# A GRU on one Trainium2 core: VectorE turns the scaled x of two time steps in one instruction instead of one

## The reference

```python
def step(h, xs):
    xzt, xrt, xht = xs                       # x @ W_z, x @ W_r, x @ W of this time step
    z = sigmoid(xzt + h @ U_z + vz)          # vz, vr, vh: condition @ C_z, C_r, C plus bias
    r = sigmoid(xrt + h @ U_r + vr)
    hh = tanh(xht + r * h @ U + vh)
    h_new = (1.0 - z) * h + z * hh
    return (h_new, h_new)
...
_, out_t = jax.lax.scan(step, h0, xs)
return x + swapaxes(out_t, 0, 1)
```

## Time and profile before

| | us |
|---|---|
| median of three runs | 2360.33 |
| lowest and highest run | 2358.73, 2360.34 |
| the profiled execution's own time | 2360.46 |
| its span, first to last instruction | 2358.3 |

### The profile page before, as it was taken

How to read it: one execution, slowest core, us unless ns; L and a number is a source line. 1 busy time by engine, 2 the same in 40 slices (tenths; PEclk the granted TensorE clock), 3 DMA queues, 4 the chain that set the end, 5 groups by cost and what they waited for, 6 DMA issues and landing times.

```text
span 2358.3 us, 186250 instructions
## 1 busy us (share of the span) xinstructions
PE 2291.0 (97%) x83078; PEld 1886.3 (80%) x83078; DVE 1750.7 (74%) x7717; ACT 1044.5 (44%) x3091; POOL 630.3 (27%) x1165
## 2 busy tenths in 40 slices
PE   2999999999999999999999999999999999999998
PEld 1788878888788887888878888888888888888887
DVE  4777777777777777777777777777777777777776
ACT  2444444444444444444444444444444444444443
POOL 0222222222222222222222222222222222222222
PEclk8999999999999999999999999999999999999999
DMA  9010110110101101101101101111011011011000
GB/s 201 20 36 18 36 36 18 36 36 18 36 24 30 36 19 36 36 18 36 36 19 36 36 18 36 27 27 36 21 33 36 18 36 36 18 36 36 18 18 21
DMA packets 145362, 78.17 MB, mean 33 GB/s; under 512 B 9024, under 2 KB 140608, under 8 KB 145216
## 3 DMA queue, kind: packets, MB, share of 16 engines
q1 hardware_dynamic: 145216, 76.84, 13.6%
HBM read 43.25 MB, written 33.55 MB: 33 GB/s over the span
## 4 chain that ended last, share of the span: by engine, by line
PE 92%; DVE 3%; SPq 2%; ACT 1%; issue 1%; DMA 1%; ACTq 0%; POOLq 0%; POOL 0%; DVEq 0%
PE banks L226 39%; PE p_bank L234 38%; PE banks L256 14%; DVE taken L533 1%; SPq L135 1%; ACT gate_c L363 1%; DVE h_t L539 1%; DVE state L537 1%; DMA u<-in_L_cond_U_dram 1%; SPq L130 0%; ACT L358 0%; PE p_bank L242 0%; SPq L145 0%; ACT L356 0%; ACT gate_r L358 0%
## 5 line engine op out<-in xcount | busy, mean ns | idle before, releaser
L234 PE MATMUL p_bank<-w_hi,x_t 128*32 128x384 f16 x16384 | 1187.7, 326 | 5.1 <-DVE w_lo L452 3.5
L234 PE MATMUL p_bank<-w_lo,x_t 128*32 128x384 f16 x8192 | 710.2, 326 | 0.0
L234 PEld LDWEIGHTS p_bank<-w_hi,x_t 128*32 128x32 f16 x16384 | 481.5, 97 | 146.6 <-issue 6.0
L226 PE MATMUL banks<-u,h_t 128*32 128x128 f32 x16384 | 548.0, 274 | 14.5 <-DMA u<-in_L_cond_U_dram 5.8
L226 PE MATMUL banks<-u,reset_t 128*32 128x128 f32 x16384 | 543.6, 273 | 5.9 <-DVE reset_t L523 4.9
L226 PEld LDWEIGHTS banks<-u,h_t 128*32 128x32 f32 x16384 | 411.9, 109 | 140.8 <-DVE h_t L539 125.2
L226 PEld LDWEIGHTS banks<-u,reset_t 128*32 128x32 f32 x16384 | 428.5, 109 | 91.7 <-DVE reset_t L523 76.0
L198 POOL TENSOR_TENSOR kept<-keep,state 128x128 f32<-128x128 f32 x512 | 234.7, 458 | 896.4 <-ACT keep L360 896.4
L430 DVE SCALAR_TENSOR_TENSOR banks<-p_bank,x_down,base 128x128 f32<-128x128 f32 x1536 | 470.2, 337 | 5.0 <-issue 3.4
L208 POOL TENSOR_TENSOR result<-x_nat,state 128x128 f32<-128x128 f32 x512 | 234.3, 458 | 817.7 <-DVE state L537 817.7
L356 ACT ACTIVATE h_hi<-h_t 128x128 f16<-128x128 f32 x512 | 158.6, 310 | 433.7 <-DVE h_t L539 433.6
(11 more groups left out here) (55 smaller groups left out, 1837.7 us busy)
## 6 DMA issues: line engine op xcount, KB each, us to landing
x_nat<-in_x_dram SPq DMA_DIRECT2D x256, 128.0 KB, 3.1
out_dram<-result SPq DMA_DIRECT2D x256, 128.0 KB, 2.7
w_stage<-in_L_cond_W_r_dram SPq DMA_DIRECT2D x4, 256.0 KB, 5.5
w_stage<-in_L_cond_W_z_dram SPq DMA_DIRECT2D x4, 256.0 KB, 8.3
w_stage<-in_L_cond_W_dram SPq DMA_DIRECT2D x4, 256.0 KB, 10.8
u<-in_L_cond_U_z_dram SPq DMA_DIRECT2D x4, 256.0 KB, 13.6
c_w<-in_L_cond_C_r_dram SPq DMA_DIRECT2D x4, 256.0 KB, 12.2
c_w<-in_L_cond_C_z_dram SPq DMA_DIRECT2D x4, 256.0 KB, 15.0
```

The source lines that it names most:

```text
L226: last = nc.tensor.matmul(out[part(j)], turned[:, part(q)], weights[:, q, cols(j)], start=first and q == 0, stop=q == Q - 1, skip_group_ch ...
L234: last = nc.tensor.matmul(p_bank[k][part(j), 0:G * N], x_t[:, c, part(q), a], w[b][:, :, q, cols(j)], start=f == 0, stop=f == GROUPS - 1, ...
```

## The change

`turn_x` takes two neighbouring places of `x_t` at once: 128x256 words in one instruction, and counts `x_t_ready` up by two. In the steps it is issued only where tt is odd, so step tt turns the x of tt + 3 and of tt + 4. In front of the loop two such instructions turn all four steps of the first set; before, three instructions turned three of them.

```diff
+    TURNS = 2
...
             def turn_x(k, c, sets):
                 dve.wait_ge(x_lo_ready, sets)
-                V.transpose(x_t[:, c].rearrange("p n a -> p (n a)").bitcast(i32),
-                            x_parts[k][:, cols(c)].rearrange("p n a -> p (n a)").bitcast(i32)).then_inc(x_t_ready, 1)
+                V.transpose(x_t[:, c:c + TURNS].rearrange("p c n a -> p (c n a)").bitcast(i32),
+                            x_parts[k][:, N * c:N * (c + TURNS)].rearrange("p n a -> p (n a)").bitcast(i32))\
+                    .then_inc(x_t_ready, TURNS)
...
-            for c in range(TURN_AHEAD):
+            for c in range(0, SET, TURNS):
                 turn_x(0, c, 1)
...
                 dve.wait_ge(kept_ready, now)
-                if not (last and tt >= STEPS - TURN_AHEAD):
+                if tt % TURNS == TURNS - 1 and not (last and tt >= STEPS - TURN_AHEAD):
                     ahead_m, c = divmod(tt + TURN_AHEAD, SET)
                     turn_x(ahead_m % 2, c, count(i * (STEPS // SET) + (ahead_m + 1)))
```

## The result

| | before | after |
|---|---|---|
| median us (6 runs each) | 2360.32 | 2370.14 |
| lowest to highest | 2358.73 to 2361.15 | 2368.40 to 2371.68 |
| span of the profiled execution | 2358.3 | 2368.5 |
| VectorE busy us, instructions | 1750.7, 7717 | 1729.7, 7461 |

The ratio is 1.0043, with a 95% interval of 1.0030 to 1.0056. The forecast was 2360.3, no change, with a range of 2355.5 to 2364.5. The measured time lies 5.6 us above that range: VectorE does less, and the kernel is slower.

The account below looks back on a forecast made before the run. TensorE was taken as the bound, with 92% of the span in the chain of waits. All terms summed to 0 on the profiled 2360.46 us; with the median 0.13 below, 2360.3 us, range 2355.5 to 2364.5.

Parts of the forecast that it names:

- No turn in even steps: VectorE before `taken`: idles 0.30 us longer, still waits for `gate_c`; the moved `kept` wait is never later; gain 0.
- theory A: From the experiments: an instruction whose last wait stands in a separate instruction in front starts 0.07 us later.
- B: From the experiments: `taken` starts later because no turn stands in front of it.
- Behind `taken` there is next to no room: TensorE after `taken`: whatever delays `taken` delays the kernel by about the same.
- The pair in odd steps: VectorE's 256-word turn: 0.41 us, 0.30 to 0.60, ending before `gate_c`; cost on the path 0.
- the pair outlasts its cover: Slower rival: a pair of 0.73 us or more delays `taken` and TensorE; 0.80 us would give 2378; chance 0.03.
- VectorE's time counts after all: Faster rival: VectorE is the bound and the saved 49 us all come back, 2311; chance 0.01.
- The turn had slowed GpSimd: Faster rival at t = 0: the turn lengthens `x_parts`; 2.4 us, at most 30; chance 0.03 beyond 4.7 us.
- The gaps in the stream: VectorE's 14 gaps of about 0.24 us move; 3.4 us either way, taken as 0; chance 0.02 better, 0.04 worse.
- the pair's own wait: VectorE's pair needs GpSimd's low halves, ready 3.5 us before it starts; nothing is needed earlier than it stands.
- ScalarE's wait: `high_x` at t = 3 waits for a turned set; the wait can only get shorter and is off the path; cost 0.
- the start: Turns before the loop: 0 to 0.2 us more, disappearing in TensorE's 5.82 us wait for a DMA of U; cost 0.

Follow-up runs that it names:

- experiment 1: Changed kernel with the two waits before `taken` in even steps swapped, so `taken` itself carries `c_gate`: 2358.36 us, ratio 0.9995 to the kernel before.
- experiment 2: Kernel before, single turns kept, with the `kept_ready` wait moved behind the turn so `taken` has two waits in every step: 2387.39 us, ratio 1.0115.
- experiment 6: Changed kernel with the two waits before `taken` swapped only in the t = 2 steps, not at t = 0: 2359.40 us, ratio 0.9993.
- experiment 7: experiment 1 with each pair turned three times, twice into scratch tiles that nothing reads: 2415.18 us, ratio 1.0228.
- experiment 5: experiment 1 and experiment 4 together (pairs, `c_gate` on `taken`, `x_parts` in halves): 2330.03 us, ratio 0.9866.
- experiment 4: Kernel before, single turns kept, with GpSimd's `x_parts` cut into two halves, in the t = 0 and t = 1 steps: 2330.87 us, ratio 0.9873.
- experiment 3: experiment 1 with one more wait instruction in each even step, on semaphores long reached: 2358.99 us, ratio 0.9995.

## Why the prediction was wrong, point by point

**The step that failed** is "No turn in even steps" of the change part by part: "The wait for `kept` now stands in front of `taken`; `kept` ends at 1016.11, 0.76 before `gate_c`, so it is never the later of the two", from which followed a gain, and a cost, of 0. The times are right and the conclusion from them was not. I asked when the moved wait is satisfied and not what it does to the instruction it lands on. It displaced the wait for `c_gate` from `taken` into an instruction of its own. Measured, the start of `taken` moved from 0.03 to 0.10 us behind `gate_c`, 0.07 in each of the 128 steps where nothing hides it. The price was on view ahead of the run: as a row with two names in its brackets, and in its size in the last three steps of the kernel before, where `taken` already starts 0.10 behind `gate_c`. Those steps have no turn either, so they can't tell theory A from B. Experiments 1, 2 and 6 show the cause: the loss goes with the order of two lines, it can be put into the kernel before, and it sits where nothing hides it.

**Where the 10 us went.** Between the two traces of before and after the span grew by 10.2. From the fifth to the sixty-first `taken` of a pass it is 250.31 against 249.60 us in the seven passes of the loop, and 0.3 more in the last, 5.3 in all. The seven joints between passes are 0.19 longer each, 1.3. The last joint has another 2.4, which holds the stop behind the loop. The start is 1.1 later (the first `taken` 0.8, the fifth 0.3 more). There TensorE waits for the DMA of U until 57.3 and not 55.7, and since the first `taken` of the ten traces lies anywhere from 59.3 to 63.5, this can't be put down to the change. In passes and joints, the 0.07 of the t = 2 steps is 9.0 us, less 1.6 for one gap in place of two per pass. Open is a rest of some 3 us between the changed kernel and experiments 1 and 6 (11.8 and 10.7 us by the medians, against 8.5 and 7.9 in passes and joints). In the traces it lies at the start and in the last joint, but for 0.2 of the last three steps. Why the stop there should be longer in the changed kernel I don't know; it isn't the pairs as such, as the last joint is 3.1 longer than the others in experiment 2, which has none, and 1.3 shorter in experiment 7.

**"Behind `taken` there is next to no room"** was right, and stricter than I used it: 70 ns are enough, as experiment 2 shows in three steps of four. With that sentence on the page I should have priced the start of `taken` to the hundredth, not only its inputs.

**The pair in odd steps** was right in its result: hidden (experiments 1 and 5). Its length was 0.445 and not 0.41. The rival "the pair outlasts its cover" has its mechanism (experiment 7) and a point of about 0.7 us. In the changed kernel one odd step per pass comes near it: a gap delays the pair, `taken` starts 0.07 to 0.08 behind `gate_c`, is 0.04 shorter, and nothing is lost.

**"VectorE's time counts after all"** was rightly set aside. Its busy time fell by 21 us, not by my 49. Some 9 of the 21 are `taken`, which starts later at t = 0 and so lasts less (179.0 to 169.7 us in all). In experiment 1, where `taken` is as before, VectorE is busy 1742.9 us, 7.8 less than before or 0.03 per pair. I counted whole instructions, but a turn overlaps the one in front of it. Where turns follow each other a single one takes 0.20 from start to start and one of 256 words 0.345 on average (experiment 7), which is 0.055 us less than two singles. The Trainium skill's fixed part for VectorE (VectorE: DVE Perf Modes, The TRN2 errata), 58 cycles or, as an estimate at its 0.96 GHz, 60 ns, agrees with that; behind a seed, as in the steps, 0.03 is left of it. None of it reaches the end, since it is saved in front of a wait.

**"The turn had slowed GpSimd"** was wrong in all sizes: `x_parts` has a median of 1.28 us without the turn inside it, as before (1.277 against 1.283). The other half of that reading, that the end of `x_parts` holds up `taken`, is shown by experiment 4, which gets 29 us back. The rule of the Trainium skill (SBUF — State Buffer, SBUF: two separate sides) that a VectorE instruction with two SBUF inputs waits for the whole of a GpSimd instruction that reads SBUF and started first agrees: `taken` ended 0.14 to 0.15 behind `x_parts` in each of the 119 or 120 sets of a trace in which it started while `x_parts` ran.

**The gaps in the stream** moved as expected and are small: 2, 1 and 0 on the path of a pass, at 0.2 us each.

**The other terms** (the pair's own wait, ScalarE's wait, the start) show no cost that the traces can tell from nothing, as predicted.

## What to carry to other kernels

- When an instruction is taken out from between two waits, look at what the waits attach to afterwards. Write the wait that is satisfied last so that it stays on the instruction that needs it, and the early ones in front.
- Where the trace shows a loop without slack, count the latency from the last input to the start of the next instruction (here 0.03 us) as a resource of its own. An instruction that is "free" behind a wait is only free if it leaves this number alone.
- Fewer and larger instructions gain nothing in front of a wait. The 29 us here lay in the length of one instruction on another engine: cutting `x_parts` in two, at 0.19 us more of GpSimd time per set (2 x 0.74 against 1.29), made room for the one that matters.

## What the runs showed of the hardware that I had not expected

- A VectorE instruction that carries the wait itself starts 0.03 us behind the end of the ScalarE instruction it waits for. With that wait in a separate instruction in front, it is 0.10, over 512 steps of experiment 2. The packed trace splits the 0.10: the separate instruction starts 0.036 behind the end of `gate_c`, lasts 0.021, and `taken` starts 0.044 behind its end. Why that last part is there is argued and not shown; the Trainium skill (Perfetto Trace Analysis, Per-engine timelines) describes that an engine's instruction is decoded ahead and waits in a queue, while an instruction of the sequencer alone is waited for before the next one is decoded. That would be this difference, and the page gives no number for it.
- A satisfied wait costs nothing that can be seen: two more of them in 256 steps (experiment 3) left `taken` of those steps at 0.03.
- A transpose of 128x256 words takes 445 ns behind a wait and follows its like after 345 ns on average (experiment 7); one that was waiting behind a busy engine is recorded shorter, at 0.40, and `taken` at 0.25 instead of 0.29.
